# Identity matmuls in TensorE's waits: a decoder layer on one core

## The chip, the core and the metric

One core of a Trainium2 chip runs the whole layer. The metric is device time in microseconds (us), from start to end of the program, as the median of three runs. The core has five engines, each with its own instruction stream: TensorE (PE: matmuls and transposes, with its weight loads shown as PEld), VectorE (DVE), ScalarE (ACT), GpSimd (POOL) and SyncE (SP, which here issues DMAs). They meet at semaphores only. TensorE's clock has two levels, 1.2 and 2.4 GHz; the profile gives the level that was granted as a share of the full one (0.50 or 1.00, and a mean where a stretch holds both).

## The reference

The input is `x`, 8 sequences of 256 tokens with 256 features. Three sublayers and a mixture of experts follow one another, each behind a norm, with residual sums:

```python
# 1. a Mamba-2 layer: projection, causal convolution of 4 taps, chunked scan, gate, norm, projection
zxbcdt = u @ in_proj_w
dt = jax.nn.softplus(zxbcdt[..., -NHEADS:] + dt_bias)
xBC = conv * jax.nn.sigmoid(conv)
y, _ = _ssd(x * dt[..., None], A[None, None, :] * dt, Bm, Cm, CHUNK)
...
# 2. cross attention to ctx_1024: 16 heads of 64, with an added mask
# 3. causal self attention: 16 query heads of 16, 4 key heads, rotary embedding
scores = jnp.where(causal, scores, -jnp.inf)
...
# 4. two of four experts for each token
h = jax.nn.silu(xf @ w1[e]) * (xf @ w3[e])
out = out + comb[:, e:e + 1] * (h @ w2[e])
```

All is in float32. The kernel keeps that precision by splitting each operand of a projection into a high part, rounded to the matmul's fast float32 form, and a low part, and by adding three products (`split_matmul`).

## The kernel before

The 2048 tokens are taken in four groups of 512 (two sequences). For each group three stages run one after the other, each in a block of its own: `stage_mamba`, `stage_cross` and `stage_attention`. `stage_experts` follows once. At the end of a block every engine waits for all the others, and only then do the instructions of the next stage begin. So TensorE's program is a fixed list; nothing is moved between stages.

In a stage, TensorE's order is written out by hand. The places that matter here are the seams, where TensorE has nothing to do until another engine is ready:

- **Mamba, before the scan.** TensorE projects six feature tiles and the gates (`win`), VectorE convolves each tile (three instructions each, line 546) and counts `conv_done`; ScalarE takes the tanh, and VectorE multiplies (line 556) and counts `conv_silu`. Then `front(0)` on TensorE transposes `a_xs` (line 396), makes the chunk's scores (403, 407), and forms the sums of decays (416), which also need `z_gated`, VectorE's four instructions of line 586.
- **Cross attention, its start.** ScalarE and VectorE split the context in parts `b_eh` and `b_el` (lines 901, 965; `context_low`), and TensorE's first work is `project_v`: products with `wv`.
- **Self attention, its start.** VectorE computes the norm's roots by a chain of small instructions and writes `c_xr` (line 1386, `y_normed`); TensorE transposes it (line 166), ScalarE and VectorE split it (`y_low`), TensorE multiplies by `aqkv` (24 products), VectorE rotates the result (lines 1407 to 1416) token tile by token tile, ScalarE and GpSimd split it (`qk_low`), TensorE transposes the keys `c_ks` (1238) and the queries `c_parts` (1195), repeats the keys by a matmul (1191), ScalarE places them (1326), and the first scores follow (1211).
- **Self attention, its end.** TensorE transposes two halves of the normed rows (line 1244, `turn_half`), each when VectorE has written it (`h_normed`). Behind the second half lies the end of the block, and behind that the next group's Mamba stage, whose first twelve products (lines 100 to 102) give the time steps and the first tile for the convolution.

`K["identr"]` is a 128x128 identity in the fast float32 form. It lies in SBUF through all groups.

Of the kernel before, what the change touches and what calls it, by code (L numbers as in the profile page):

```python
# [13 lines left out]
P = 128  # L14
# [4 lines left out]
NG = TOK // (P * GT)  # L19
GN = GT * P  # L20
# [5 lines left out]
CT = XT + 2  # L26
# [134 lines left out]
def transposes_in(pe, src, ident, banks, tiles, ready, done):  # L161

    for t in range(GT):
        pe.wait_ge(ready, t + 1)
        for k in range(tiles):
            ins = pe.transpose(banks[k][:, t * P:(t + 1) * P], src[:, t, k * P:(k + 1) * P], ident)
            if t == GT - 1:
                ins.then_inc(done, 1)


def part_high(act, out, psum, scale=None):
# [118 lines left out]
def stage_mamba(nc, ctx, g, I, W, K, XN, XG, CX, ps, s, last):  # L290


    with ExitStack() as own:
# [11 lines left out]
        v, r, e, den, zz, z2, acc, dt, a = (sb(n, [P, GT, NH]) for n in "v r e den zz z2 acc dt a".split())  # L305
# [45 lines left out]
        def _(pe):  # L351
# [34 lines left out]
            def front(t):  # L386
                c = t % QT

                if t == 0:
                    pe.wait_ge(s["conv_silu"], CT)  # L390
                    if g:
                        pe.wait_ge(s["logits_copied"], 1)
                if t >= 2:
                    pe.wait_ge(s["x_times_dt"], t - 1)
                for k in range(XT):
                    ins = pe.transpose(T[t % 2][:, k * P:(k + 1) * P], xs[:, k, t * P:(t + 1) * P], ident)
                ins.then_inc(s["x_turned"], 1)

                if t == 0:
                    pe.wait_ge(s["decay_rates"], 1)  # L400
                else:
                    pe.wait_ge(s["small_bank_read"], t)
                pe.matmul(SM[:, 0:P], xs[:, XT, t * P:(t + 1) * P], xs[:, XT + 1, t * P:(t + 1) * P], start=True, stop=True)
                if c:
                    pe.matmul(SM[:, P:2 * P], xs[:, XT, (t - 1) * P:t * P], xs[:, XT + 1, t * P:(t + 1) * P],
                              start=True, stop=True)
                ins = pe.matmul(SM[:, 2 * P:2 * P + NH], upto if c else after, a[:, t, :], start=True, stop=True)
                ins.then_inc(s["chunk_scores"], 1)

                pe.wait_ge(s["decays_masked"], t + 1)  # L410
                for i, bank in enumerate(DB):
                    if t:
                        pe.wait_ge(s["decays_exp"], 2 * t - 1 + i)
                    elif i == 0:
                        pe.wait_ge(s["z_gated"], GT)
                    ins = pe.matmul(bank[:], after, av[:, t % 2, i * HH:(i + 1) * HH, :], start=True, stop=True)
                    ins.then_inc(s["decay_sums_half"], 1)
                pe.wait_ge(s["decay_sums_half"], 2 * t + 2)
                pe.sem_inc(s["decay_sums"], 1)
# [246 lines left out]
def stage_cross(nc, ctx, g, W, K, XG, CX, KL, ps, s, last):  # L666
    with ExitStack() as own:  # L667
# [92 lines left out]
        def _(pe):  # L760
# [74 lines left out]
                ins.then_inc(s["heads_turned"], 1)  # L835


            pe.wait_ge(s["context_low"], 1)
            for n in range(4):
                project_v(n)  # L840
# [226 lines left out]
def stage_attention(nc, ctx, g, I, W, K, XN, XG, RAW, rows_of, ps, s, weights_in, last):  # L1067

    weights, at_rows, at_out = rows_of
    with ExitStack() as own:  # L1070
# [62 lines left out]
        @block.sync  # L1133
        def _(sp):

            sp.dma_start(XN[:], I["x"][(g + 1) % NG]).then_inc(s["next_x_in"], 16)
            clear(sp, last)
            if g == NG - 1:
                w13, w2 = RAW
                for e in range(NE):  # L1140
                    sp.dma_start(w13[:, e, :, 0:HID], weights["w1"][e]).then_inc(weights_in, 16)
                    sp.dma_start(w13[:, e, :, HID:UP - MID], weights["w3"][e][:, :, MID:HID]).then_inc(weights_in, 16)
                    sp.dma_start(w13[:, e, :, UP - MID:UP], weights["w3"][e][:, :, 0:MID]).then_inc(weights_in, 16)
                    sp.dma_start(w2[:, e], weights["w2"][e]).then_inc(weights_in, 16)
            sp.wait_ge(s["residual_added"], GT)
            sp.dma_start(at_out[g], XG[:]).then_inc(s["stored"], 16)
            sp.wait_ge(s["h_normed"], GT)
            sp.dma_start(at_rows[g], xr[:]).then_inc(s["stored"], 16)
# [22 lines left out]

        @block.tensor
        def _(pe):
            transposes_in(pe, xr, ident, TB, KD, s["y_normed"], s["y_turned"])
            pe.wait_ge(s["y_low"], KD)

            for t in range(GT):
                for k in range(KD):
                    ins = split_matmul(pe, ps[t][:, 0:AQKV], (uh[:, k, t * P:(t + 1) * P], ul[:, k, t * P:(t + 1) * P]),
                                       [w[:, k, :] for w in W["aqkv"]], k == 0, k == KD - 1)  # L1180
                ins.then_inc(s["qkv_projected"], 1)
            pe.wait_ge(s["qk_low"], 2 * GT)

            def build(i):

                m, what = i // 3, i % 3
                bank = BANKS[i] if i < 3 else BB
                if i >= 3:
                    pe.wait_ge(s["built_placed"], i)
                if what:  # L1190
                    pe.matmul(bank[:], repeat[:, 2 * m + what - 1].rearrange("p a d -> p (a d)"), kT[:], start=True,
                              stop=True).then_inc(s["built_ready"], 1)
                    return
                for t in range(GT):
                    ins = pe.transpose(bank[:, t * P:(t + 1) * P].bitcast(FR), qs[:, t, m].rearrange("p a b -> p (a b)"), identr)
                ins.then_inc(s["built_ready"], 1)

            def scores(n):
                m, b, r = where(n)
                if n % PER == 0:  # L1200
                    pe.wait_ge(s["built_placed"], 3 * m + 3)
                if n == 0:
                    pe.wait_ge(s["q_masked_by_scalar"], FIRST)
                if n % PER < REP and n >= FIRST:
                    pe.wait_ge(s["q_masked"], REP * m + r + 1 - FIRST)
                if n >= 3:
                    pe.wait_ge(s["scores_masked"], 2 * (n - 2))
                for qt in range(QT):
                    at, w = (b * QT + qt) * P, (qt + 1) * P
                    for part in range(2):  # L1210
                        ins = pe.matmul(SB[n % 3][:, qt * P:qt * P + w], qv[:, m % 2, r, at:at + P],  # L1211
                                        kv[:, m % 2, part, b * S:b * S + w], start=part == 0, stop=part == 1)
                ins.then_inc(s["scores_ready"], 1)
# [36 lines left out]
            pe.wait_ge(s["k_copied"], 1)  # L1250
            for i in range(3):
                build(i)
            scores(0)
            scores(1)
            for n in range(NHD + 1):
# [38 lines left out]
            project(3)  # L1294

            for hf in range(2):
                pe.wait_ge(s["h_normed"], QT * (hf + 1))
                turn_half(hf, xr, TB[1 - hf], s["h_turned"])

        @block.scalar  # L1300
        def _(act):
# [669 lines left out]
```

## Time and profile before

| | |
|---|---|
| median of three runs | 1479.81 us (1479.68 to 1483.67) |
| profiled execution, its span from the first to the last instruction | 1475.8 us |
| what lies around the span, by the median | 4.0 us |
| TensorE busy in the span | 1223.5 us (83%) |
| VectorE busy | 958.9 us (65%) |
| ScalarE busy | 677.2 us (46%) |
| GpSimd busy | 262.4 us (18%) |
| mean granted TensorE clock | 0.909 |

The page gives no time of the profiled execution besides its span, so the 4.0 us are the median less the span. A busy TensorE does not tell at which of its two clocks it worked: the same matmul counts for more busy time at the lower one. The granted clock has to be read beside it.

### The profile page before, as it was taken

How to read it: one execution, taken by the hardware profiler on the slowest of the kernel's cores; microseconds unless marked ns; L12 is line 12 of the kernel's file. 1: busy time of each engine (PE TensorE's matmuls, PEld its weight loads, DVE VectorE, ACT ScalarE, POOL GpSimd, SP SyncE). 2: the span in 40 equal slices, each digit the busy share in tenths (PEclk: the TensorE clock that was granted, in tenths of full speed). 3: DMA queues.
4: the chain of work that ended last, by engine and by line, in shares of the span. 5: the costliest groups of instructions: out<-in, count | busy, mean ns of one | idle time of the engine just before them, and what ended most of it. 6: DMA issues, size and time to landing. Idle time of an engine off the chain costs nothing. (4 is left out here: it accounts for less than half of the span.)

```text
span 1475.8 us, 24651 instructions
## 1 busy us (share of the span) xinstructions
PE 1223.5 (83%) x8122; PEld 1088.3 (74%) x8122; DVE 958.9 (65%) x2994; ACT 677.2 (46%) x1498; POOL 262.4 (18%) x267
## 2 busy tenths in 40 slices
PE   0888996978799697888987969799597159999997
PEld 0567996956699696667986957699596148888886
DVE  5665766676567656766766676577656975555553
ACT  4625644735266175625635745366274403333331
POOL 3100003310000150100003310000150612333332
PEclk9899997989899889899997988999798559999999
DMA  5005510010263001006510010263510001222221
GB/s 206 29 1 128 126 35 14 1 58 1 57 140 90 15 1 30 29 1 140 133 29 1 1 58 1 67 148 73 222 50 32 0 15 30 37 37 39 40 38 22
DMA packets 45258, 80.34 MB, mean 54 GB/s; under 512 B 8432, under 2 KB 18160, under 8 KB 44496
## 3 DMA queue, kind: packets, MB, share of 16 engines
q1 hardware_dynamic: 36976, 69.19, 17.4%
q0 software_dynamic: 6720, 9.18, 3.9%
q8 instruction: 70, 1.15, 0.3%
q10 hardware_dynamic: 1440, 0.39, 0.1%
q14 instruction: 52, 0.43, 0.1%
HBM read 28.01 MB, written 8.78 MB: 25 GB/s over the span
## 5 line engine op out<-in xcount | busy, mean ns | idle before, releaser
L945 ACT ACTIVATE b_pp<-b_pp,b_nm 128x256 f32<-128x256 f32 x256 | 116.0, 501 | 87.0 <-DVE b_nm L983 86.1
L824 PEld LDWEIGHTS bank<-b_va,b_pt 128*128 128x128 f32 x1024 | 127.7, 191 | 4.1
L824 PE MATMUL bank<-b_va,b_pt 128*128 128x65 f32 x1024 | 128.5, 269 | 0.0
L1233 PE MATMUL bank<-c_v,c_pt 128*128 128x68 f32 x768 | 101.5, 269 | 0.1
L1211 PE MATMUL bank<-c_kv,c_qv 128*128 128x128 f32 (+1 forms) x512 | 95.5, 316 | 7.4 <-ACT c_kv L1326 7.4
L1169 POOL TENSOR_SCALAR c_qv<-c_rot,const 128x512 fp32r<-128x512 f32 x56 | 87.2, 1575 | 77.9 <-ACT c_rot L1322 77.9
L1233 PEld LDWEIGHTS bank<-c_v,c_pt 128*128 128x128 f32 x768 | 98.3, 193 | 1.7 <-DVE c_pt L1433 0.7
L983 DVE CUSTOM_DVE_ANT_0 b_pp<-bank,mask 128x256 f32<-128x256 f32 x256 | 96.9, 417 | 0.0
L100 PE MATMUL bank<-e_up_low,e_xh 128*128 x210 | 89.7, 427 | 1.8 <-DVE e_xl L178 1.8
L1696 ACT ACTIVATE e_th<-bank 128x512 f32<-128x512 f32 x35 | 21.0, 601 | 146.4 <-PE bank L102 146.4
L1425 DVE CUSTOM_DVE_ANT_0 c_pp<-bank,const 128x128 f32<-128x128 f32 (+1 forms) x256 | 80.1, 350 | 9.5 <-PE bank L1211 9.5
L1152 POOL MEMSET c_v<- 128x16 f32 x4 | 0.5, 127 | 474.4 <-POOLq L667 474.4
L811 PE MATMUL bank<-const,b_pp 128*128 128x128 f32 x512 | 78.5, 276 | 7.6 <-ACT b_pp L945 7.5
L1592 POOL DMA_INDIRECT out<-e_ys,e_ids x35 | 55.5, 1586 | 164.5 <-DVE e_ys L1827 160.3
L102 PE MATMUL bank<-e_up_high,e_xh 128*128 x210 | 84.3, 401 | 0.0
L101 PE MATMUL bank<-e_up_high,e_xl 128*128 x210 | 83.6, 398 | 0.0
L797 PE MATMUL bank<-k_low_twice,b_qst 128*128 128x256 f32 x256 | 76.3, 322 | 7.7 <-DMA b_qst<-b_ql 7.7
L1810 DVE SCALAR_TENSOR_TENSOR e_th<-e_th,bank 128x512 f32<-128x512 f32 x70 | 38.8, 554 | 65.8 <-ACT e_th L1696 57.1
L1211 PEld LDWEIGHTS bank<-c_kv,c_qv 128*128 128x128 f32 x512 | 73.3, 209 | 10.2 <-ACT c_kv L1326 10.2
L178 DVE SCALAR_TENSOR_TENSOR b_ql<-bank,b_qst 64x512 fp32r<-64x512 f32 x64 | 44.1, 689 | 53.6 <-ACT b_qst L916 30.5
L546 DVE SCALAR_TENSOR_TENSOR a_cv<-bank,taps,a_cv 128x510 f32<-128x510 f32 (+2 forms) x72 | 53.3, 740 | 35.4 <-ACT a_cv L478 33.7
L1336 ACT ACTIVATE c_pp<-c_pp,c_nm 128x128 f32<-128x128 f32 x128 | 51.5, 402 | 49.8 <-DVE c_nm L1425 49.8
(372 smaller groups left out, 3591.2 us busy)
## 6 DMA issues: line engine op xcount, KB each, us to landing
b_kst<-b_kh SPq DMA_DIRECT2D x128, 128.0 KB, 2.3
k_low_twice<-b_kl SPq DMA_DIRECT2D x128, 128.0 KB, 2.4
b_qst<-b_ql SPq DMA_DIRECT2D x64, 128.0 KB, 2.3
raw_up<-in_w SPq DMA_DIRECT2D x4, 768.0 KB, 10.2
raw_down<-in_w SPq DMA_DIRECT2D x4, 768.0 KB, 12.1
XN<-in_x SPq DMA_DIRECT2D x5, 512.0 KB, 3.4
context<-in_ctxT SPq DMA_DIRECT2D x4, 512.0 KB, 5.7
mask<-in_mask SPq DMA_DIRECT2D x4, 512.0 KB, 6.6
```

The costliest lines, as they stand in the source:

```text
L100: pe.matmul(out, ah, bl, start=start, stop=False)
L101: pe.matmul(out, al, bh, start=False, stop=False)
L102: return pe.matmul(out, ah, bh, start=False, stop=stop)
L797: pe.matmul(out, qst[:, j % 2, hp, tokens(b, qt)], klst[j % 2][:, hp, b * S:(b + 1) * S], start=True, stop=False)
L811: ins = pe.transpose(T2[n % 2][:, kt * S + qt * P:kt * S + (qt + 1) * P], pp[:, n % 3, qt, kt * P:(kt + 1) * P], ident)
L824: ins = pe.matmul(O2[u % 2][:, at:at + VW], pt[:, n % 2, kt * S + qt * P:kt * S + (qt + 1) * P], va[:, b * QT + kt, 2 * j + hp, :], start= ...
L945: act.activation(pp[:, n % 3, qt, :], pp[:, n % 3, qt, :], ACT.Exp, bias=nm[:, n % 4, qt:qt + 1], scale=-1.0).then_inc(s["probs_exp"], 1)
L983: dve.tensor_tensor_reduce(out=pp[:, n % 3, qt, :], in0=S3[n % 3][:, qt * S:(qt + 1) * S], in1=mask[:, b * QT + qt, :], scale=-1.0, scalar ...
L1169: pool.tensor_scalar(qv[:, m % 2, r, :], qb, rows(r), None, ALU.mult).then_inc(s["q_masked"], 1)
L1211: ins = pe.matmul(SB[n % 3][:, qt * P:qt * P + w], qv[:, m % 2, r, at:at + P], kv[:, m % 2, part, b * S:b * S + w], start=part == 0, stop= ...
L1233: ins = pe.matmul(OB[u % 2][:, at:at + AKV * AVW], pt[:, n % 4, i * P:(i + 1) * P], v[:, b * QT + kt].rearrange("p a b -> p (a b)"), start ...
L1425: dve.tensor_tensor_reduce(out=pp[:, n % 4, w], in0=SB[n % 3][:, w], in1=causal[:, (QT - 1 - qt) * P:QT * P], scale=-AD ** -0.5, scalar=3e ...
```

## The change

A new helper, `keep_busy`, issues `n` matmuls of the identity with itself, each 512 columns wide (the 128 columns of the identity four times), into a PSUM bank that nobody reads at that time. It is called at eight places of TensorE's program in each group of 512 tokens: 9 in the Mamba stage, 9 in cross attention, 16, 10, 24, 7, 12 and 10 in self attention; the last 10 are left out in the last group. That is 97 in a group and 378 in all. Ahead of the 9 in the Mamba stage stands a new wait, for the last `conv_done`. Nothing is taken away, and the experts are as they were.

```diff
+def keep_busy(pe, bank, K, n):
+
+    for _ in range(n):
+        pe.matmul(bank[:].rearrange("p (a b) -> p a b", b=P), K["identr"][:],
+                  K["identr"][:].unsqueeze(1).to_broadcast([P, GN // P, P]), start=True, stop=True)
...
                 if t == 0:
+                    pe.wait_ge(s["conv_done"], CT)
+                    keep_busy(pe, SM, K, 9)
                     pe.wait_ge(s["conv_silu"], CT)
...
+            keep_busy(pe, O2[0], K, 9)
             pe.wait_ge(s["context_low"], 1)
...
+            keep_busy(pe, OB[1], K, 16)
             transposes_in(pe, xr, ident, TB, KD, s["y_normed"], s["y_turned"])
+            keep_busy(pe, OB[1], K, 10)
             pe.wait_ge(s["y_low"], KD)
...
+            keep_busy(pe, OB[1], K, 24)
             pe.wait_ge(s["qk_low"], 2 * GT)
...
+            keep_busy(pe, TB[0], K, 7)
             scores(0)
...
             for hf in range(2):
+                if hf:
+                    keep_busy(pe, OB[1], K, 12)
                 pe.wait_ge(s["h_normed"], QT * (hf + 1))
                 turn_half(hf, xr, TB[1 - hf], s["h_turned"])
+            if g < NG - 1:
+                keep_busy(pe, OB[1], K, 10)
```

The order of TensorE's instructions at the start of the first cross attention, before the change (a row is an instruction or a run of the same ones, with the semaphores that it waits for; `a_` names belong to the Mamba stage, `b_` to cross attention):

```order
L102 MATMUL bank<-wout_high,a_yh 128x256
L293 UNCONDITIONAL_BRANCH
L759 UNCONDITIONAL_BRANCH [waits barrier_Pool_Activation_PE_DVE_SP_release]
L100 MATMUL bank<-wv_low,b_eh 128x512 [waits b_context_low]
L101 MATMUL bank<-wv_high,b_el 128x512
```

And of the change at the same place:

```order
L102 MATMUL bank<-wout_high,a_yh 128x256
L300 UNCONDITIONAL_BRANCH
L768 UNCONDITIONAL_BRANCH [waits barrier_Pool_Activation_PE_DVE_SP_release]
L174 MATMUL bank<-identr 128x512 x9
L100 MATMUL bank<-wv_low,b_eh 128x512 [waits b_context_low]
L101 MATMUL bank<-wv_high,b_el 128x512
```

The nine identity matmuls stand behind the wait of all engines for one another, and wait for nothing themselves.

TensorE's order in the change around the third and fourth call in self attention, where the 24 lie between the last product with `aqkv` and the transposes of the keys, and the 7 between the repeated keys and the first scores:

```order
L102 MATMUL bank<-aqkv_high,uh 128x384
L174 MATMUL bank<-identr 128x512 x24
L1251 MATMUL bank<-identr,c_ks 128x128 [waits c_qk_low]
L1251 MATMUL bank<-identr,c_ks 128x128 x3
L1208 MATMUL bank<-identr,c_parts 128x128 [waits c_k_copied,c_repeat_set,c_ones_set]
L1208 MATMUL bank<-identr,c_parts 128x128 x3
L1204 MATMUL bank<-c_kT,c_repeat 128x512 x2
L174 MATMUL bank<-identr 128x512 x7
L1224 MATMUL bank<-c_kv,c_qv 128x128 [waits c_q_masked_by_scalar,c_built_placed]
```

Before the change the same rows stand there without the two of line 174; lines 1251, 1208, 1204 and 1224 are 1238, 1195, 1191 and 1211 of the kernel before.

## Rows read from the trace of the kernel before

**Rows 1.** The page: the span.

```profile
span 1475.8 us, 24651 instructions
```

**Rows 2.** Who TensorE waited for, 37.5 to 1137.4: us in total, times, longest.

```profile
PE bank L166 <- DVE c_xr L1386: 22.2, 4, 5.6
PE bank L100 <- DVE b_el L965: 21.5, 4, 5.4
PE bank L1244 <- DVE c_xr L1480: 21.0, 8, 4.0
PE bank L1238 <- POOL c_ks L1161: 18.5, 4, 4.8
...
PE bank L797 <- DMA b_qst<-b_ql: 7.7, 5, 1.9
```

**Rows 3.** Stretches: length, busy us (instructions) by engine, granted clock, DMA share, GB/s.

```profile
55.80:61.20 5.40, 0.04 (x1) 0.04 (x1) 5.20 (x9) 3.34 (x8) 0.51 (x3) 0.72 0.00 2
...
98.80:102.50 3.70, 0.01 (x1) 0.00 (x0) 2.31 (x8) 0.69 (x1) 0.21 (x1) 1.00 0.00 0
...
104.20:109.30 5.10, 5.10 (x12) 4.04 (x13) 3.26 (x17) 0.60 (x1) 0.00 (x0) 0.50 0.00 0
...
120.00:200.00 80.00, 76.25 (x576) 71.47 (x574) 55.88 (x206) 49.61 (x101) 0.00 (x0) 1.00 0.57 132
...
224.00:232.20 8.20, 6.19 (x21) 5.76 (x22) 5.19 (x14) 1.52 (x3) 0.00 (x0) 0.50 0.00 0
...
239.10:249.30 10.20, 7.51 (x35) 6.63 (x36) 5.80 (x31) 6.49 (x14) 3.44 (x4) 0.50 0.00 0
...
311.80:317.50 5.70, 5.67 (x16) 3.08 (x16) 0.00 (x0) 0.94 (x2) 0.00 (x0) 0.50 0.96 319
```

```profile
376.00:382.40 6.40, 4.03 (x10) 3.16 (x11) 4.55 (x18) 1.66 (x2) 0.20 (x1) 0.50 0.01 4
```

**Rows 4.** TensorE in order of time, first `project_v`: start, us, instruction, idle before.

```profile
104.18 0.79 PE L100 MATMUL bank<-wv_low,b_eh 128*128 128x512 f32 x1 [5.37 <-DVE b_el L965]
...
105.62 0.63 PE L100 MATMUL bank<-wv_low,b_eh 128*128 128x512 f32 x1
106.05 0.63 PE L101 MATMUL bank<-wv_high,b_el 128*128 128x512 f32 x1
...
109.65 0.39 PE L101 MATMUL bank<-wv_high,b_el 128*128 128x512 f32 x1
109.88 0.40 PE L102 MATMUL bank<-wv_high,b_eh 128*128 128x512 f32 x1
```

**Rows 5.** In order of time, the first instructions behind each kind of block end.

```profile
101.79 0.21 POOL L757 MEMSET b_va<- 128x64 f32 x1 [45.32 <-POOLq L293]
...
220.13 0.17 DVE L1381 TENSOR_SCALAR c_nt<-moments 128x4 f32<-128x4 f32 x1 [0.55 <-PEq L667]
...
311.83 0.58 PE L100 MATMUL bank<-ul,win_high 128*8 128x512 f32 x1 [2.12 <-PEq L1070]
```

**Rows 6.** TensorE in self attention: the first transposes and the first scores.

```profile
224.00 1.97 PE L166 MATMUL bank<-const,c_xr 128*128 128x128 f32 x8 [5.56 <-DVE c_xr L1386]
...
244.24 2.93 PE L1211 MATMUL bank<-c_kv,c_qv 128*128 128x128 f32 x12 [1.84 <-ACT c_kv L1326]
```

**Rows 7.** VectorE: the rotation of the second and third token tile.

```profile
232.22 0.49 DVE L1407 TENSOR_TENSOR c_ra<-bank,rope 128x320 f32<-128x320 f32 x1 [0.31 <-PE bank L102]
...
233.88 0.48 DVE L1407 TENSOR_TENSOR c_ra<-bank,rope 128x320 f32<-128x320 f32 x1
```

**Rows 8.** The Mamba seam of the first group, VectorE and TensorE.

```profile
59.64 1.47 DVE L556 SCALAR_TENSOR_TENSOR a_xs<-a_th,a_cv 128x512 f32<-128x512 f32 x2
```

```profile
61.16 1.11 PE L396 MATMUL bank<-const,a_xs 128*128 128x128 f32 x4 [5.37 <-DVE a_xs L556]
...
63.64 3.75 PE L416 MATMUL bank<-a_av,const 128*128 128x512 f32 x4 [0.71 <-DVE a_zg L586]
...
69.00 1.96 PE L416 MATMUL bank<-a_av,const 128*128 128x512 f32 x4
```

## The prediction

> **What bounds the kernel now.** I read the page first for the span, 1475.8 us [rows 1], and TensorE's mean granted clock, 0.909: some of its work runs at half speed. Next I read who TensorE waits for [rows 2]. Five waits come back in each of the four groups: 5.6 us for the first normed rows of self attention, 5.4 us for the split context, 4.0 us for the second half of the last norm, 4.8 us for the split keys, and 5.4 us ahead of the scan [rows 8]. They are waits for VectorE, ScalarE and GpSimd, and the change does not make those engines faster. What it can give is the second cost of such a wait: behind it TensorE works at half its clock. The stretches show it [rows 3]. From 98.8 to 102.5 TensorE idles at clock 1.00; its work from 104.2 to 109.3 is dense and at 0.50. From 224.0 to 232.2, from 239.1 to 249.3 and from 311.8 to 317.5 it is the same. One matmul of 512 columns shows the price [rows 4]: 0.427 us from start to start at the low clock (105.62 to 106.05), 0.232 at the high one (109.65 to 109.88). So each such matmul costs 0.195 us more behind a seam.
>
> When does the clock fall? In the first cross attention it was still high at 102.5, 3.7 us after TensorE's last product near 98.8; in the second group it was low from 376.0 on. The mean of 0.72 over 55.8 to 61.2 puts the fall near 58.2, that is 2.4 us after the last work [rows 3]. The waits for a DMA, up to 1.9 us [rows 2], left no low stretch: one lies in the 80 us from 120.0 with a mean clock of 1.00 [rows 3]. So a rest under 2 us is taken to be safe, one of 3 to 4 us as open, and one over 5 us as lost. When does it rise? Dense work at the low clock lasted 5.2 us from 104.2 and 5.7 us from 311.8; in the second group the clock was back at 382.4 [rows 3].
>
> **The change part by part.** An identity matmul has the form of the products that were priced, 512 columns of fast float32, so I cost it at 0.232 us high and 0.427 us low. The weights are loaded for each, as in those rows, under the matmul before. Ninety-seven in a group are 22.5 us at the high clock. What lies on the path depends on the wait that each call fills.
>
> *Start of self attention, 16 and 10.* The block begins at 220.1 [rows 5]; the transposes began at 224.0 [rows 6], 3.9 us later. Sixteen take 16 x 0.232 = 3.7 us, so they end at 223.8: hidden. TensorE's rest before them is what was left of the stage before, 220.1 less 218.4 (5.56 us before 224.0), 1.7 us: safe, so the clock stays high. The eight transposes took 1.97 us at the low clock [rows 6]; VectorE hands over the rows tile by tile, so only the end of them shortens, and of the 1.0 us that half the time would save I take 0.4. The ten take 2.3 us and fill the 2.0 us in which ScalarE and VectorE split the rows (225.97 to about 228.0); they cost 0.0 to 0.3, and I take nothing, for the transposes end earlier. The products with `aqkv` then run high. VectorE's second tile waited for them at 232.22, its third did not and followed after 1.66 us [rows 7]. With the first tile ready at half the time (six products of 384 columns), the second follows it at VectorE's pace and no longer at TensorE's; by the pitch this pulls the chain of VectorE forward by about 1.2 us (384 columns are three quarters of the pitch above: twelve products at 0.32 us are 3.9 us; six at 0.17 us and one tile of 1.66 us are 2.7). Sum: 1.6 us in each group, ends 0.5 and 2.0.
>
> *The 24 and the 7.* Twenty-four are 5.6 us. The wait for the split keys was 4.8 us behind products that ended, all of them, some 2.3 us later than they will [rows 2, 3]; the keys come 1.6 us earlier. So the room is about 5.5 us: hidden to within 0.2. The seven are 1.6 us in a wait of 1.84 us [rows 6]. Here the clock was low for 10.2 us with 7.51 us of TensorE's work in it [rows 3]. The first part of that work (transposes, repeats) hangs between steps of ScalarE, so I give it 0.3 us. From 244.24 on TensorE worked without a pause for 5.1 us; at the high clock that is half, but the first heads also go through VectorE and ScalarE. Between 0.5 and 2.5 us I take 1.2. Sum 1.5 us in each group. If the clock fell all the same, the 24 would cost 24 x 0.427 = 10.2 us against a room of 5.5.
>
> *End of self attention, 12 and 10, and the next group's start.* Twelve are 2.8 us in a wait of 4.0 us [rows 2]. The rest left is 1.2 us: safe. The four transposes behind it get 0.5 us faster. The ten are 2.3 us, in a rest of 2.12 us before 311.83 [rows 5] that has itself become shorter; I take 0.25 us off the gain. Then the twelve first products of the Mamba stage, up to 12 x 0.195 = 2.3 us, on which the convolution's chain on VectorE hangs. Some groups had part of them at the high clock already, so 2.0. Sum 2.25 us, three times (the fourth group has no such seam): 6.8 us.
>
> *Start of cross attention, 9.* The block begins at 101.8 [rows 5], the first product at 104.18 [rows 4]. The room is 2.3 us, and nine take 2.1 us at the high clock, but the rest before them is 3.0 us, and the clock was still high only until 102.5. So three run high and six low: 0.7 + 2.6 us, and `project_v` starts at 105.1, 0.9 us late. In return the dense work began 2.3 us earlier. The rises above came 4 to 6 us after dense work began, so the clock is back at 106 to 108: two to seven low products in place of twelve, 10 x 0.195 = 2.0 or 5 x 0.195 = 1.0 us, less 0.9. That is 0.1 to 1.1. If the clock never falls, all twelve are saved: 2.3 us. I take 1.0, four times: 4.0 us.
>
> *Ahead of the scan, 9.* The new wait holds them back until the last convolution is done, at about 59.7, since VectorE's next two instructions start at 59.64 [rows 8]. The first transposes began at 61.16. Room 1.4 us; the clock fell at about 58.2, so all nine are low, 3.8 us, and `front(0)` comes 2.4 us late, behind it ScalarE and VectorE of the first chunk. But line 416 waited 0.71 us for the gates anyway, and its four matmuls took 3.75 us low and take 1.96 high [rows 8]: 1.8 us back if the clock has returned by about 65.4, which 4 to 6 us of dense work from 59.8 gives. So: -2.4 + 0.7 + 1.8 = 0.1, and what follows until 69.0 (transposes and scores of the next chunk) is faster by 0.4 to 0.6. I take 0.6, ends -1.7 and 2.2 (clock never low), four times: 2.4 us.
>
> Sum: 4 x (1.6 + 1.5) + 6.8 + 4.0 + 2.4 = 25.6 us. The profiled span 1475.8 becomes 1450.2; with the 4.0 us around it, and against the median of 1479.8, the time is 1454.2 us. A third of the kernel's length, the experts, gets nothing.
>
> **A rule weighed.** The rows show that dense products bring the clock back, and the transposes from 224.0 stood at 0.50 all through [rows 3, 6]. The Trainium skill, "TensorE: Matmul & The Clock Gate", Part 4 (PE-mode transpose), says that transposes do not count as activity as matmuls do. By that rule the transposes between two calls lengthen the rest, from nothing to 1.2 us in self attention; it stays under what the rows call safe, so the sum would be the same. Part 1 of the same page says that another limiter depends on the data, zeros not tripping it; of the gate that matters here it says only that it watches how busy the array is. No row here has a product of mostly zeros that brought the clock up.
>
> **The rivals.**
>
> 1. *The identity's data does not count as activity.* 127 of 128 of its elements are zeros, and no row tests it. Then the clock falls as before, and each call that begins more than some 3.5 us after real work runs low. Late by room against cost: 16 at the start of self attention, half of them low, +1.4; 10 low (4.3 us in 2.0) +2.3; 24 partly low +1.5; 7 low (3.0 in 1.8) +1.2; 10 at the end +2.2; cross attention +1.0 to 1.6; the scan's +1.8. That is about 11.4 us in a group, 44 in all: 1524 us. For it: the array's inputs hardly toggle. Against: nothing but that the page speaks of how busy the array is. It decides when more than a third of the identity matmuls run low: the rooms of a group add up to 23.0 us (3.9 + 2.0 + 5.5 + 1.8 + 4.0 + 2.1 + 2.3 + 1.4), all high they take 22.5 and all low 41.4 us, and a third of the 18.9 between is the 6.4 us that a group is to gain.
>
> 2. *More is held.* The clock also stays high at the two open seams, cross attention and the scan: 4 x (2.3 - 1.0) + 4 x (2.2 - 0.6) = 11.6 us more, 1442.6 us. For it: the rest before the nine of cross attention is 3.0 us, and one of 3.7 us left the clock high until its end. Against: the fall at 2.4 us.
>
> 3. *Half is held or half is absorbed.* The starts of a stage are chains through ScalarE, VectorE and the DMAs; if the first scores and the convolution's chain do not follow TensorE, or one call in self attention is too long by 1 to 2 us in each group, 4 x 1.5 + 6 = 12 us go missing: 1466 us.
>
> 4. *Nothing.* Late starts eat all at each seam: 1478 us. The mixed seams show how (0.9 us late for 1.0 to 2.0 us back), but in self attention every call fits its room.
>
> **How the numbers follow.** The sum as worked out 0.57, rival 2 0.12, rival 3 0.16, rival 4 0.05, rival 1 0.10. Predicted is 1454.2 us. The range must leave out no more than 0.2: it takes in rivals 2 and 3 in full, from 1441 to 1469 us. Under 0.3% (4.4 us) a measurement of this kernel cannot tell from no change, its three runs being 4 us apart. Faster takes the sum and rivals 2 and 3, 0.85; same 0.05; slower 0.10.
>
> **What would show it.** In the profile after: line 174 with 378 matmuls, most of them 0.23 us apart; granted clock 1.00 from 220 us through the first scores, and at the start of the second Mamba stage; TensorE's mean clock at 0.95 or more; waits of line 166, 1238 and 1244 for VectorE and GpSimd shrunk to parts of a us, without VectorE waiting longer for TensorE. Still low stretches of 3 to 7 us at the scan and at cross attention in most groups. The stage of self attention about 3.3 us shorter, Mamba about 2.6 and cross attention 1.0. The prediction is wrong if the granted clock is low while identity matmuls run back to back for 7 us (rival 1), if the first real product behind a call starts over 1 us later than its operand is ready in self attention, or if the clock is high and VectorE's chain has not moved.

## The result, and the profile after

The changed kernel takes 1443.95 us (median of four runs, 1442.89 to 1444.53) against 1479.86 us before (1479.68 to 1483.67): a ratio of 0.9763, with a 95% interval of 0.974 to 0.9786. That is 35.9 us less, where 25.6 were predicted; the time lies in the range, near the rival in which more is held (1442.6 us).

The page of the changed kernel: span, busy time of TensorE, its granted clock in 40 slices (tenths), and the row of the identity matmuls with what ended the idle time before them.

```profile
span 1441.1 us, 25407 instructions
...
PE 1269.0 (88%) x8500; PEld 1123.7 (78%) x8500; DVE 959.7 (67%) x2994; ACT 675.8 (47%) x1498; POOL 263.5 (18%) x267
...
PEclk9999999999999999999999999999998559999999
...
L174 PE MATMUL bank<-identr 128*128 128x512 f32 x378 | 101.0, 419 | 27.0 <-PEq L300 12.0
```

TensorE is busy for 45.5 us more and the span is 34.7 us shorter. The slices are 9 tenths or more up to the experts; the mean granted clock went from 0.909 to 0.961. The mean of 419 ns is the time of one matmul from its start to its end; they start closer together, as the order of time below shows.

Who TensorE waited for in the changed kernel, 37.5 to 1110:

```profile
PE bank L174 <- PEq L300: 12.0, 4, 3.0
PE bank L1257 <- DVE c_xr L1498: 10.0, 8, 1.3
PE bank L174 <- DVE a_cv L555: 8.2, 4, 4.0
...
PE bank L174 <- PEq L676: 6.7, 4, 1.7
```

Of the waits in [rows 2], the first four are gone or cut: no wait is left at line 166, nor for the split context, nor for the split keys, and line 1257 (1244 before) waits 10.0 us instead of 21.0. In their place stand two rests of 3.0 and 1.7 us ahead of identity matmuls, until all engines have met, and one until the last convolution: 4.0 us in the first group and 1.4 in the others.

The stages of the first two groups of the changed kernel, between the meetings of all engines (stretch, length, busy time by engine, granted clock, DMA):

```profile
37.70:101.90 64.20, 55.47 (x295) 41.90 (x295) 44.59 (x90) 30.38 (x74) 5.75 (x19) 0.95 0.05 17
101.90:217.80 115.90, 110.39 (x801) 102.10 (x801) 76.51 (x260) 60.62 (x119) 0.21 (x1) 1.00 0.40 92
217.80:305.80 88.00, 81.69 (x603) 74.83 (x603) 63.77 (x291) 49.98 (x121) 27.72 (x24) 1.00 0.03 10
305.80:368.00 62.20, 56.11 (x319) 43.83 (x319) 44.59 (x90) 30.56 (x75) 5.74 (x19) 0.95 0.09 30
368.00:484.00 116.00, 110.46 (x801) 102.09 (x801) 76.51 (x260) 60.55 (x119) 0.22 (x1) 1.00 0.40 92
484.00:572.00 88.00, 81.70 (x603) 74.84 (x603) 63.79 (x291) 49.95 (x121) 27.73 (x24) 1.00 0.03 10
```

The same stages of the kernel before:

```profile
37.50:101.70 64.20, 53.34 (x286) 39.50 (x286) 44.55 (x90) 30.47 (x74) 5.74 (x19) 0.92 0.05 17
101.70:220.00 118.30, 110.51 (x792) 102.23 (x792) 76.59 (x260) 60.53 (x119) 0.21 (x1) 0.97 0.39 90
220.00:311.70 91.70, 69.43 (x524) 66.18 (x524) 63.59 (x291) 50.26 (x121) 27.33 (x24) 0.86 0.03 10
311.70:375.90 64.20, 55.92 (x310) 42.55 (x310) 44.51 (x90) 30.54 (x75) 5.73 (x19) 0.90 0.09 30
375.90:495.60 119.70, 111.93 (x792) 103.76 (x792) 76.58 (x260) 60.56 (x119) 0.21 (x1) 0.94 0.39 89
495.60:587.60 92.00, 70.21 (x524) 66.99 (x524) 63.59 (x291) 50.35 (x121) 27.54 (x24) 0.87 0.03 9
```

In this execution self attention and cross attention run at 1.00 from end to end. The first row at the start of cross attention, to which others are compared below:

```profile
101.98 2.30 PE L174 MATMUL bank<-identr 128*128 128x512 f32 x9 [3.01 <-PEq L300]
```

Over all four groups, self attention is 15.4 us shorter (3.7, 4.1, 3.3, 4.3), cross attention 11.6 (2.4, 3.7, 2.9, 2.7), Mamba 6.7 (0, 1.9, 1.5, 3.2), and the experts 1.2. VectorE, ScalarE and GpSimd do the same work in the same time in each stage: only TensorE's clock and its rests differ.

### The profile page after: what moved, and what is told of

It reads as the page before. It is cut to its first block and busy times, and to the rows that moved or that the text cites. A ratio compares the mean times of both kernels' runs of the same rounds, so it can differ in the third digit from the quotient of the medians.

```text
span 1441.1 us, 25407 instructions
## 1 busy us (share of the span) xinstructions
PE 1269.0 (88%) x8500; PEld 1123.7 (78%) x8500; DVE 959.7 (67%) x2994; ACT 675.8 (47%) x1498; POOL 263.5 (18%) x267
## 5 line engine op out<-in xcount | busy, mean ns | idle before, releaser
L174 PE MATMUL bank<-identr 128*128 128x512 f32 x378 | 101.0, 419 | 27.0 <-PEq L300 12.0
L174 PEld LDWEIGHTS bank<-identr 128*128 128x128 f32 x378 | 74.0, 201 | 44.0 <-issue 20.2
L1224 PE MATMUL bank<-c_kv,c_qv 128*128 128x128 f32 (+1 forms) x512 | 88.4, 298 | 2.7 <-ACT c_kv L1344 2.7
L1828 DVE SCALAR_TENSOR_TENSOR e_th<-e_th,bank 128x512 f32<-128x512 f32 x70 | 38.8, 554 | 65.6 <-ACT e_th L1714 56.9
```

The source lines that it names most:

```text
L174: pe.matmul(bank[:].rearrange("p (a b) -> p a b", b=P), K["identr"][:], K["identr"][:].unsqueeze(1).to_broadcast([P, GN // P, P]), start=T ...
```

## The experiments

Each kernel ran beside the kernel before on the same chip; ratios are to it. The kernel before had medians from 1477.3 to 1479.9 us in these comparisons, so a difference of 2 us between two changed kernels of different comparisons is not clear of noise. Each trace is one execution. What is changed is work whose results nobody reads, in some kernels also the new wait ahead of the scan, and once a scratch write.

**One seam at a time.** Three kernels keep the calls of one stage alone.

```diff
 (only_self)
-                    pe.wait_ge(s["conv_done"], CT)
-                    keep_busy(pe, SM, K, 9)
...
-            keep_busy(pe, O2[0], K, 9)
```

only_self: 

> Only the six calls in self attention are kept (306 of 378 identity matmuls); the calls in cross attention and ahead of the scan, and the new wait, are gone. Theory A, each seam gives back its own low stretches and the gains add up: the change made the four self attention stages 15.4 us shorter in all and the three Mamba starts behind them some 6 us, so about 22 us faster than before, 1458 us (ratio 0.985). Rival B, the attention gain needs the clock to be held in the stages around it: under 15 us, and low stretches come back inside self attention.

Measured: 1455.16 us, ratio 0.9845 (0.9821 to 0.9868), 22.9 us less. Theory A holds: all self attention stages are 88.0 us (87.6 in the last group) and without a low stretch, as in the full change, and the three Mamba stages behind them are 62.9 to 63.1 us.

only_cross: 

> Only the nine at the start of cross attention are kept (36 matmuls). Theory A, a rest of 3.0 us ahead of the nine always holds the clock: no low stretch at the start of cross attention in any group, each of these stages about 115.9 us instead of 118.3 to 119.7, 11 to 12 us faster than before, 1468 us. Rival B, whether a rest of 3.0 us makes the clock fall depends on where in time it lies, and the stages now start at other times than in the changed kernel: the clock falls in two or three of the four groups, and the gain is 5 to 9 us, 1471 to 1475 us.

Measured: 1470.46 us, ratio 0.9951 (0.9936 to 0.9966), 7.6 us less. Theory A falls. B's gain of 5 to 9 us came, but not its count of groups: the clock fell at the start of cross attention in all four, 0.6 to 0.9 us into the stage, while in the full change it fell in none, with the same rest of 3.0 us. Still the stages took 117.2 to 117.5 us, not 118.3 to 119.7. The low stretch was half as long (3.4 us, and 6.8 before).

only_scan: 

> Only the wait for the last convolution and the nine behind it, ahead of the scan, are kept (36 matmuls). Theory A, the nine begin when the clock is already low, start the scan over 3 us late and give back about as much: within 2 us of before, 1478 to 1482 us. Rival B, they bring the clock back earlier and the rest of the scan gains: 3 to 6 us faster, 1474 to 1477 us.

Measured: 1468.94 us, ratio 0.9938 (0.9915 to 0.9961), 9.1 us less: theory A falls, and the gain is beyond B's 3 to 6 us too. The four Mamba stages took 63.3 us, 4.4 us less in all. The rest, again some 4.5 us, lies in stages that this kernel doesn't touch (cross attention took 118.1 us in each group where it had taken up to 119.7, the experts 1.3 us less): the low stretches lay elsewhere in this execution, and why is not shown. So a part of any one-seam result is not that seam's.

**The same kernel, started later.**

```diff
+        pad = own.enter_context(nc.sbuf_tensor("w_pad", [P, 2, 1024], F32))
...
+            for i in range(2):
+                pool.memset(pad[:, i], 0.0)
```

> The changed kernel with two memsets of scratch on GpSimd behind the loading of the weights, where GpSimd is the last engine: all that follows starts 1 to 3 us later, and nothing else changes. Theory A, rests of 3.0 us are safe wherever they lie: the changed kernel's time plus the memsets, 1445 to 1447 us, and no low stretch at cross attention. Rival B, it depends on where they lie in time: low stretches come at the start of cross attention in some or all groups, 1 to 2.5 us each, 1449 to 1456 us.

Measured: 1445.17 us, ratio 0.9775 (0.9752 to 0.9799); the first group begins 1.9 us later. Theory A has the time right and theory B the clock. The second cross attention of this kernel, TensorE in order of time:

```profile
370.36 3.88 PE L174 MATMUL bank<-identr 128*128 128x512 f32 x9 [3.01 <-PEq L303]
374.07 0.40 PE L100 MATMUL bank<-wv_low,b_eh 128*128 128x512 f32 x1
374.31 0.40 PE L101 MATMUL bank<-wv_high,b_el 128*128 128x512 f32 x1
```

And two stretches of it, cross attention and the Mamba stage ahead of it:

```profile
370.30:487.50 117.20, 111.78 (x801) 103.31 (x801) 76.60 (x260) 60.49 (x119) 0.22 (x1) 0.99 0.39 91
309.30:370.30 61.00, 54.78 (x319) 42.74 (x319) 44.58 (x90) 30.52 (x75) 5.73 (x19) 0.97 0.09 31
```

After the same rest of 3.0 us the nine took 3.88 us instead of 2.30: now the clock did fall. But it was back as the real products began, which start 3.8 us into the stage, not 2.5, and run 0.23 us apart. The price is 1.3 us and not a low stretch of products. In return the low stretch at the scan is 3.4 us long and no longer 6.8, and the Mamba stage 61.0 us and not 62.2. The third and fourth group are like this. In the first, cross attention took 118.5 us, with a second low stretch of 6.8 us from 128.2 on. What one seam loses the other wins: over the four groups Mamba is 4.9 us shorter than in the changed kernel and cross attention 6.3 us longer, and the total, less the 1.9 us, is the changed kernel's to within a us.

That the later start is the cause is not shown. The next kernel (dense data) starts its groups within 0.7 us of the changed kernel's times, and from the second group on it has the same low stretches as this one. The moment at which the clock falls is no fixed one even behind the same instructions. Ahead of the first scan all three kernels run the same program on TensorE and rest 4.0 us. These are the rests, first in the changed kernel, then in the one with dense data, then in the one started later:

```profile
56.40:60.30 3.90, 0.00 (x0) 0.00 (x0) 3.79 (x7) 1.90 (x3) 0.51 (x2) 0.86 0.00 2
56.80:60.80 4.00, 0.06 (x1) 0.00 (x0) 3.89 (x7) 1.89 (x3) 0.58 (x3) 0.94 0.01 2
57.70:61.70 4.00, 0.01 (x1) 0.00 (x0) 3.89 (x7) 1.91 (x4) 0.54 (x3) 0.78 0.01 2
```

By their mean clocks of 0.86, 0.94 and 0.78 it fell 2.8, 3.5 and 2.2 us after TensorE's last product. So a rest of 3.0 us can end with the clock high or low, and one trace of a kernel shows one outcome of it. The four executions of the changed kernel had mean clocks from 0.959 to 0.963, and so had those of the later start. Over the five kernels that have the nine behind such a rest (the change, this one, only_cross, dense_data, eight_more) the clock fell at 14 of 20 starts of cross attention.

**The data.**

```diff
-        pe.matmul(bank[:].rearrange("p (a b) -> p a b", b=P), K["identr"][:],
-                  K["identr"][:].unsqueeze(1).to_broadcast([P, GN // P, P]), start=True, stop=True)
+        pe.matmul(bank[:], K["dense"][:, 0, 0:P], K["dense"][:].rearrange("p k d -> p (k d)"), start=True, stop=True)
```

> The changed kernel with products of dense weights (the high part of awo, 128x128 stationary and 512 columns moving) in place of identity by identity; same count, places and shape. Theory A, the data does not matter to the clock: 1443 to 1446 us, the same low stretches by place. Rival B, zeros count for less: with dense data the clock is also held at the scan or at cross attention, and the time is 3 us or more below the changed kernel's.

Measured: 1443.57 us, ratio 0.9766 (0.9743 to 0.9788), the same as the change. Theory A's time holds: zeros or dense weights, it is the same, and self attention has no low stretch in either. Its other half fails, for the low stretches lie elsewhere: the clock fell at the start of cross attention in all four groups, as here in the second,

```profile
367.31 3.89 PE L174 MATMUL bank<-awo_high 128*128 128x512 f32 x9 [3.03 <-PEq L299]
```

and at the scan it was low for 3.4 us and not 6.8. Mamba takes 5.0 us less than in the changed kernel over the four groups, and cross attention 5.1 more. From the second group on this is the pattern of the later start, without its shift. B's gain of 3 us or more did not come.

**The form.** Two short instructions in place of each wide one, first as transposes, then as matmuls.

```diff
-    for _ in range(n):
...
+    for i in range(2 * n):
+        pe.transpose(bank[:, i % 4 * P:(i % 4 + 1) * P].bitcast(FR), K["identr"][:], K["identr"][:])
```

by_transposes: 

> The changed kernel with two transposes of the identity (128 columns each, rounded float32) in place of each identity matmul of 512 columns, at the same places: about the same length at the high clock (0.11 us each) with a quarter to a half of the columns. Theory A, transposes do not count as activity as matmuls do: the clock falls at all seams as before the change, the transposes then take 0.2 us each and lie partly on the path, 1478 to 1500 us. Rival B, a busy TensorE counts whatever it does: 1443 to 1447 us, no low stretch in self attention.

Measured: 1457.36 us, ratio 0.9846 (0.9815 to 0.9876). TensorE in the first self attention of this kernel:

```profile
220.98 2.92 PE L174 MATMUL bank<-identr 128*128 128x128 f32 x32 [1.68 <-PEq L675]
224.87 1.41 PE L166 MATMUL bank<-const,c_xr 128*128 128x128 f32 x8 [0.96 <-DVE c_xr L1403]
...
232.79 4.26 PE L174 MATMUL bank<-identr 128*128 128x128 f32 x48
238.44 0.54 PE L1250 MATMUL bank<-identr,c_ks 128*128 128x128 f32 x4 [1.39 <-POOL c_ks L1170]
...
243.08 2.93 PE L1223 MATMUL bank<-c_kv,c_qv 128*128 128x128 f32 x12 [0.63 <-ACT c_kv L1343]
```

Neither theory: the clock is held through the first half (the eight real transposes take 1.41 us, not 1.97 as in [rows 6]). This is the stretch from the start of the stage to the first product, in which TensorE does nothing but transposes:

```profile
221.00:228.40 7.40, 5.98 (x60) 5.33 (x60) 6.95 (x24) 1.27 (x2) 1.05 (x2) 1.00 0.22 72
```

The clock is 1.00 in it in all four groups. It is lost behind the 48 transposes, at 240.8, so that the first scores take 2.93 us as before the change. There two things differ from the changed kernel, the form and a rest of 1.39 us that the shorter filler left ahead of the keys; this run does not part them.

short_matmuls: 

> The control for the run with transposes: two identity matmuls of 128 columns in place of each one of 512, so as many instructions and the same 128 columns in each as there, but matmuls. Theory A, transposes as such count for less: these matmuls hold the clock in self attention as the changed kernel's do, 1443 to 1448 us. Rival B, it was the short form and not the transposing: low stretches in self attention at the same place as with transposes (about 20 us into the stage), 1452 to 1460 us.

```diff
+        pe.matmul(bank[:, i % 4 * P:(i % 4 + 1) * P], K["identr"][:], K["identr"][:], start=True, stop=True)
```

Measured: 1486.07 us, ratio 1.0046 (1.0031 to 1.0062): slower than without any identity matmul. The same place:

```profile
223.11 4.80 PE L174 MATMUL bank<-identr 128*128 128x128 f32 x32 [1.68 <-PEq L675]
227.71 1.93 PE L166 MATMUL bank<-const,c_xr 128*128 128x128 f32 x8
229.29 4.51 PE L174 MATMUL bank<-identr 128*128 128x128 f32 x20
...
238.89 5.47 PE L174 MATMUL bank<-identr 128*128 128x128 f32 x48
```

TensorE works without a pause, and the clock falls under its hands: the 32 take 4.80 us, the real transposes begin 4.7 us into the stage and not 4.0, the twenty take 4.5 us where the wait has room for 2, and the stage lasts 97.4 us in the first two groups. In these two groups short matmuls held the clock worse than short transposes, so transposing as such is not what loses it here. What differs between the three forms is seen in the start to start time for 128 columns: 0.058 us in a wide matmul, 0.09 us in a transpose, 0.11 us in a short matmul at the high clock (5.47 us for 48). In the last two groups of the short matmuls the same stage took 90.2 and 87.9 us: the clock held there through the first scores, where with transposes it fell in all four groups. So the order of the two forms is shown for half of the groups only, and why those held is left open.

**The count.** Twenty-four for the 16, and then half of every count.

```diff
-            keep_busy(pe, OB[1], K, 16)
+            keep_busy(pe, OB[1], K, 24)
```

> The changed kernel with 24 in place of the 16 at the start of self attention, in each of the four groups. Theory A, the 16 fill the wait to within 0.1 us and each further one lies on the path at 0.232 us: 8 x 0.232 x 4 = 7.4 us over the changed kernel, 1451 us, each self attention stage 1.9 us longer. Rival B, there is slack behind them (the chain through VectorE sets the pace): under 3 us over, at most 1447 us.

Measured: 1447.68 us, ratio 0.98 (0.9774 to 0.9826), 3.7 us over the changed kernel, between the two. TensorE at the start of self attention, 217.95 us:

```profile
218.06 5.74 PE L174 MATMUL bank<-identr 128*128 128x512 f32 x24 [1.68 <-PEq L676]
223.63 1.03 PE L166 MATMUL bank<-const,c_xr 128*128 128x128 f32 x8
```

and of the changed kernel, from 217.80 us:

```profile
217.91 3.91 PE L174 MATMUL bank<-identr 128*128 128x512 f32 x16 [1.68 <-PEq L676]
221.79 1.41 PE L166 MATMUL bank<-const,c_xr 128*128 128x128 f32 x8
222.95 2.54 PE L174 MATMUL bank<-identr 128*128 128x512 f32 x10
225.36 0.44 PE L100 MATMUL bank<-aqkv_low,uh 128*128 128x384 f32 x1
```

The eight begin to cost at once, 1.7 us of their 1.9 (the transposes begin 5.6 us after the first identity matmul, not 3.9), but the transposes no longer wait for VectorE's tiles (1.03 against 1.41 us). The stage is 1.3 us longer, 5.1 us in all. Mamba gave back 3.3 us, with shorter low stretches at the scan, and cross attention lost 2.5, for the clock fell at its start in two of the four groups.

```diff
-    for _ in range(n):
+    for _ in range(n // 2):
```

> The changed kernel with half of each count (4, 4, 8, 5, 12, 3, 6 and 5). Theory A, the clock needs most of each wait filled: with half, rests of 2 to 3.5 us stay in every wait, the clock falls again in self attention in some or all groups, and about half of the change's gain is left, 1456 to 1465 us. Rival B, half is enough: 1443 to 1448 us, no low stretch in self attention.

Measured: 1455.42 us, ratio 0.9855 (0.9838 to 0.9871): a little under two thirds of the gain. In the first self attention:

```profile
230.22 2.90 PE L174 MATMUL bank<-identr 128*128 128x512 f32 x12
235.86 0.54 PE L1251 MATMUL bank<-identr,c_ks 128*128 128x128 f32 x4 [2.73 <-POOL c_ks L1171]
237.17 0.50 PE L1208 MATMUL bank<-identr,c_parts 128*128 128x128 f32 x4 [0.78 <-ACT c_kT L1348]
...
238.04 1.40 PE L174 MATMUL bank<-identr 128*128 128x512 f32 x3
240.50 2.93 PE L1224 MATMUL bank<-c_kv,c_qv 128*128 128x128 f32 x12 [1.05 <-ACT c_kv L1344]
```

Theory A, 0.6 us under its range: behind rests of 2.73 and 0.78 us close together the clock fell, at 238.1, and the first scores are slow again. Self attention takes 89.0 to 89.4 us.

**No rests.** TensorE also works ahead of the scan from the start of the wait, and at the end of the Mamba stage.

```diff
-                    pe.wait_ge(s["conv_done"], CT)
-                    keep_busy(pe, SM, K, 9)
+                    keep_busy(pe, SM, K, 12 if g else 22)
...
+            keep_busy(pe, T[0], K, 12)
```

> The changed kernel with TensorE also busy in its two open rests: ahead of the scan the wait for the last convolution is gone and the count is 22 in the first group and 12 in the others (behind the gate's products), and 12 stand at the end of the Mamba stage, ahead of the meeting of all engines. Theory A, the clock then never falls before the experts and the identity matmuls stay hidden: Mamba stages of about 60 us in place of 62.3 (62 in place of 64.2 in the first group), 1434 to 1437 us. Rival B, what the scan gets back is absorbed by its chains, or the 22 or the 12 lie on the path: 1442 to 1446 us.

Measured: 1438.19 us, ratio 0.9731 (0.9709 to 0.9754), 5.8 us under the changed kernel's median and 5.4 under that of dense_data, which ran in the same comparison. It is 1.2 us over theory A's range. The first scan:

```profile
55.52 5.15 PE L174 MATMUL bank<-identr 128*128 128x512 f32 x22
61.05 0.66 PE L404 MATMUL bank<-const,a_xs 128*128 128x128 f32 x4 [0.38 <-DVE a_xs L565]
...
63.53 1.95 PE L424 MATMUL bank<-a_av,const 128*128 128x512 f32 x4 [1.48 <-DVE a_zg L595]
```

The scan starts on time, and line 416 of before takes 1.95 us: the Mamba stages are 61.8 and then 60.5 us. Against theory A the clock still fell in two groups in the middle of cross attention, around the wait for a DMA and the first scores behind it, and once at a scan.

dma_wait_too adds seven ahead of the first scores of cross attention, last_group_too also the ten at the end of the last self attention:

```diff
+            keep_busy(pe, S3[2], K, 7)
             scores(0)
...
-            if g < NG - 1:
-                keep_busy(pe, OB[1], K, 10)
+            keep_busy(pe, OB[1], K, 10)
```

> The kernel with no rests, and seven identity matmuls more in cross attention, into a bank of the scores ahead of the first scores, where TensorE waits 1.8 us for a DMA. In the kernel with no rests the clock fell there in two of four groups, and these stages took 117.3 and 117.7 us where the others took 115.8 and 115.9. Theory A, the wait for the DMA was the rest that made it fall: all four stages at 115.9 us, 3 us less, 1435 us. Rival B, the seven lie on the path or the low stretch has another cause: 1438 us or more.

Measured: 1439.72 us, ratio 0.9736 (0.9723 to 0.9749): no gain. The clock fell in three of four groups, 27.5 to 28.7 us into cross attention, now behind the wait, in the first heads. The wait for the DMA alone is not the cause; what is was not found.

> As the kernel that fills the DMA wait too, and the ten at the end of self attention also in the last group, ahead of the experts, whose 24 products with the gate took 5.25 us at the low clock and take 2.73 at the high one in the other groups. Theory A, the clock is held through the gate's products: 2.5 us less at the start of the experts and 0.3 us more in the last self attention, 1433 us. Rival B, the clock falls during them anyway, since each is 4 columns wide: within 0.5 us of the kernel without.

Measured: 1436.72 us, ratio 0.972 (0.9707 to 0.9733), the fastest of all. The experts' stage takes 334.4 us in place of 337.2. Its first products, here

```profile
1099.33 2.54 PE L174 MATMUL bank<-identr 128*128 128x512 f32 x10
1102.16 0.24 PE L100 MATMUL bank<-gate_low,c_parts 128*128 128x4 f32 x1 [0.30 <-PEq L1081]
1102.27 0.25 PE L101 MATMUL bank<-gate_high,c_parts 128*128 128x4 f32 x1
```

are 0.11 us apart, and 0.21 us in the changed kernel. Theory A's mechanism holds: 3.0 us under the kernel without, where 2.2 were expected. Its 1433 us rested on 1435 for that kernel, which took 1439.72.

## Why the prediction was right, and where its sizes were off

By place the sum was 13.2 + 6.0 + 4.0 + 2.4 us: self attention, the next group's start, cross attention, the scan. The traces show 15.4, 4.5, 11.6 and 2.2, and 1.2 in the experts. So 7.6 of the 9.3 us by which they exceed the forecast lie in cross attention.

**Start of self attention.** Right, with its numbers. The 16 ended where the transposes could begin (221.79), the 10 covered the split, `aqkv` began without a rest at 225.36, and the 24 ended at 235.3, where the transposes of the keys followed at once. VectorE's rotation shows the chain that was to move:

```profile
226.72 0.49 DVE L1425 TENSOR_TENSOR c_ra<-bank,rope 128x320 f32<-128x320 f32 x1 [1.41 <-PE bank L102]
...
228.24 0.48 DVE L1425 TENSOR_TENSOR c_ra<-bank,rope 128x320 f32<-128x320 f32 x1
```

Its second tile follows the first and waits no longer for TensorE, as in [rows 7] it did. The first scores take

```profile
239.99 1.65 PE L1224 MATMUL bank<-c_kv,c_qv 128*128 128x128 f32 x12 [0.67 <-ACT c_kv L1344]
```

1.65 us against 2.93 in [rows 6]. The terms 1.6 + 1.5 in each group and 0.25 in three were 13.2 us; measured 15.4.

**The next group's start.** 2.0 us in each of three groups was taken. The kernel with the six calls of self attention alone has Mamba stages of 62.9 to 63.1 us there, with a long low stretch at the scan; before they were 64.2, 63.8 and 65.6. That is 4.5 us in all, not 6.0, in stages whose scan also varies by a us.

**Start of cross attention.** The term that was mis-sized: 4 x 1.0 us, measured 11.6 us. The step was that the clock falls in the rest of 3.0 us, as at 102.5 [rows 3]. In the changed kernel it fell in no group, and the nine ran high. This was luck of that execution: the later start and the run with dense data have the same rest, and the clock fell in all four groups of each. There cross attention is 5.3 and 6.5 us shorter than before, where 4.0 were predicted, and Mamba 11.6 and 11.7 instead of 6.7. Where the clock fell the price was about 1.3 us a group (2.5 in the first group of the later start, with its second low stretch). Even then the loss was smaller than I had it, since the clock was back before or soon after the first product, after 3.4 us; I had read 4 to 6 us from low stretches that began with rests in them. Another 1.4 us of the 11.6 lies in the second group's stage, 119.7 us before, which had a low stretch in its middle. Here a step failed outright: I wrote that the waits for a DMA left no low stretch, from one stretch of 80 us in the first group. In the second group of the same trace the clock was low for 6.8 us, from 402.9 on, behind that very wait.

**Ahead of the scan.** Predicted 0.6 us a group. In the first group the nine ran low from 60.35 and ended at 64.4, so `front(0)` began 3.2 us late and not 2.4, and the clock was back at 66.1, as line 416's matmuls began (65.92, 2.02 us). In the first group the two cancelled: 64.2 us before and after. In the others the stage is 0.7 us under the kernel without these nine. The mechanism and the size are right for this execution, and the version without the wait shows what the place was worth: 1.8 us more in each group (2.4 in the first), by holding the clock and not by bringing it back.

**The rivals.** That the identity's zeros do not count is refuted by the changed kernel itself: from 217.9 to 235.3 TensorE did little but identity matmuls and the `aqkv` products, at a clock of 1.00. The run with dense data adds that the time is the same. That more is held came true for cross attention in this execution, and not for the scan. The experts' 1.2 us were not foreseen. The 4.0 us around the span were too many: the changed kernel's profiled execution took 1442.89 us with a span of 1441.1, which leaves 1.8. The trace of before is of an execution about 2 us under its median. The saving of 25.6 us does not hang on this, only 1454.2 does, by about 2 us. With 1478 us the loss side was never near, but the short matmuls show that it exists: identity work that does not hold the clock made the kernel 0.5% slower, by the lateness that rival 1 was priced with.

**The rule weighed.** The Trainium skill, "TensorE: Matmul & The Clock Gate", Part 4, has transposes not counting as matmuls do. Here 60 transposes and nothing else over 7.4 us, behind a rest of 1.7 us, kept the clock at 1.00 in all four groups, so for keeping it, in this form (rounded float32, 128 columns), the trace does not bear the rule out. No run here shows whether transposes alone bring a low clock back.

## What to carry to other kernels

A wait costs twice when the engine behind it has a clock that falls: look for dense work at 0.50 behind each seam, and price it by the same instruction at both levels in the same trace. Unread work in the wait buys the second cost back if it begins as soon as the rest begins, is as wide as the real products (as it was where it worked best here), and ends just before the operand arrives; too little leaves the fall, too much or too sparse lies on the path. The meeting of all engines at a stage's end is itself a rest. Filled behind the meeting alone, 3.0 us of it were left, and the clock fell at 14 of 20 starts of cross attention; filled ahead of it as well, 0.3 us were left, and the clock fell at none of 12 (the three kernels without rests). Filling ahead was not run alone, so its part of the gain is not known. And one trace is one outcome: when the same rest leaves the clock high in one trace and low in another, compare the sum over all seams and not one seam.

## What was not expected

The same rest of 3.0 us cost the clock in all four groups of three kernels, in two groups of one and in none of the changed kernel, while the total of kernels with the same fillers stayed the same to within a us or two. What decides it is not shown; the later start was meant to be the cause, and the run with dense data shows the same pattern without it. Against the picture that each seam has a price of its own, a low stretch moved from one seam to another. And back to back matmuls of 128 columns, without a pause on TensorE, did not keep its clock in two of four groups.
